# Key-row gathers of a two-layer Perceiver kernel: one transfer per chunk and half, or two of eight heads each

## The reference

```python
x = x + _L0_xattn_ref(_layernorm(x), ctx, mask, ...)   # cross-attention, 4 heads of 64
x = x + _L0_attn_ref(_layernorm(x), ...)               # gated delta net, 12 heads
x = x + _L0_ffn_ref(_layernorm(x), ...)                # 8 experts, top 1
x = x + _L1_xattn_ref(_layernorm(x), ctx, ...)         # cross-attention, 16 heads of 16
x = x + _L1_attn_ref(_layernorm(x), ...)               # linear attention with decay
x = x + _L1_ffn_ref(_layernorm(x), ...)                # 8 experts, top 2
```

## Time and profile before

| | us |
|---|---|
| median of 3 runs | 948.26 (947.57 to 948.73) |
| the profiled execution | 944.76 |
| its span in the profile | 943.0 |
| TensorE matmuls busy | 899.3 (95%) |
| VectorE busy | 704.8 (75%) |
| ScalarE busy | 487.5 (52%) |
| GpSimd busy | 300.1 (32%) |
| HBM read and written | 81.48 and 53.07 MB |

### The profile page before, as it was taken

How to read it: one execution, slowest core, us unless ns; L and a number is a source line. 1 busy time by engine, 2 the same in 40 slices (tenths; PEclk the granted TensorE clock), 3 DMA queues, 4 the chain that set the end, 5 groups by cost and what they waited for, 6 DMA issues and landing times. The chain is left out here.

```text
span 943.0 us, 21457 instructions
## 1 busy us (share of the span) xinstructions
PE 899.3 (95%) x8230; PEld 580.0 (62%) x8230; DVE 704.8 (75%) x1216; ACT 487.5 (52%) x1156; POOL 300.1 (32%) x435
## 2 busy tenths in 40 slices
PE   8999999999999999999999989989999999999987
PEld 5444554455445545567788856666667666776675
DVE  3499888988898889997577448768778788887426
ACT  2543454345434544344583413556667666666742
POOL 5564346434643464445065127201100000000100
PEclk9999999999999999999999979999999999999999
DMA  9467855575356535533300078786666667766000
GB/s 171 171 185 211 250 183 171 143 186 183 104 143 186 180 103 158 132 117 119 134 1 1 1 186 215 203 210 163 163 164 164 163 176 185 177 180 187 5 3 6
DMA packets 103655, 136.33 MB, mean 145 GB/s; under 512 B 64152, under 2 KB 85424, under 8 KB 100880
## 3 DMA queue, kind: packets, MB, share of 16 engines
q1 hardware_dynamic: 99856, 134.22, 52.3%
q10 hardware_dynamic: 3712, 0.92, 0.6%
HBM read 81.48 MB, written 53.07 MB: 143 GB/s over the span
## 5 line engine op out<-in xcount | busy, mean ns | idle before, releaser
L1974 DVE TENSOR_REDUCE mx<-bank 128x1 f32<-128x896 f32 x224 | 232.9, 1086 | 54.6 <-PE bank L1818 53.1
L2035 ACT ACTIVATE p<-bank 128x512 f32<-128x512 f32 x392 | 202.9, 602 | 103.7 <-PE bank L1861 103.4
L704 DVE STREAM_TRANSPOSE ew<-sc 32x896 f32<-32x896 f32 x208 | 229.3, 1102 | 15.3 <-ACT sc L788 7.7
L563 PE MATMUL bank<-Wv,ctxT 128*128 128x512 f32 (+1 forms) x336 | 146.4, 575 | 0.0
L1861 PE MATMUL bank<-home,krows 99*128 99x128 bf16 x1568 | 124.7, 220 | 7.7 <-issue 3.4
L1861 PEld LDWEIGHTS bank<-home,krows 99*128 99x128 bf16 x1568 | 101.3, 98 | 46.4 <-issue 9.9
L1818 PE MATMUL bank<-krows,home 96*128 96x512 bf16 x448 | 123.0, 355 | 1.7 <-DMA krows<-kscr 0.9
L1874 PE MATMUL bank<-p,v 128*32 128x128 f32 x3136 | 108.0, 276 | 3.2 <-issue 3.1
L563 PEld LDWEIGHTS bank<-Wv,ctxT 128*128 128x128 f32 x336 | 63.6, 190 | 71.6 <-issue 64.1
L1874 PEld LDWEIGHTS bank<-p,v 128*32 128x32 f32 x3136 | 80.8, 110 | 31.3 <-ACT p L2035 23.0
L445 POOL CAST kt<-kf 128x512 bf16<-128x512 f32 (+1 forms) x56 | 31.3, 558 | 203.3 <-ACT kf L760 203.3
(11 more groups left out here) (317 smaller groups left out, 1158.1 us busy)
## 6 DMA issues: line engine op xcount, KB each, us to landing
krows<-kscr SPq DMA_DIRECT2D x14, 1536.0 KB, 9.9
krows<-kscr SPq DMA_DIRECT2D x14, 1152.0 KB, 14.7
v<-vscr SPq DMA_DIRECT2D x14, 1004.5 KB, 13.8
vscr<-vpair SPq DMA_DIRECT2D x12, 1004.5 KB, 4.0
kscr<-kt SPq DMA_DIRECT2D x14, 768.0 KB, 3.6
kscr<-kt SPq DMA_DIRECT2D x14, 576.0 KB, 5.1
kscr<-kt SPq DMA_DIRECT2D x14, 512.0 KB, 4.5
ctxB<-ctx SPq DMA_DIRECT2D x56, 112.0 KB, 4.0
```

Of the source, the lines that this page charges most:

```text
L563: ins = pe.matmul(bank[kv_bank(op, s)][:, 0:w * D], turned_context(c)[:, i, k * P:(k + 1) * P], Wv01[:, i, 0:w].rearrange("p w o -> p (w o)"),
L704: dve.transpose(pT0[j * SQ:(j + 1) * SQ, :, :, i * SQ:(i + 1) * SQ].rearrange("m t h q -> m h t q"), rows[:, j]).then_inc(S("turn0"), 1)
L1974: dve.tensor_reduce(mx1[:, c % 2, h:h + 1], psum[:, b:b + 2, :].rearrange("p b n -> p (b n)")[:, 0:CH], AX.X, ALU.max).then_inc(S("smread1 ...
L2035: act.activation(p1[:, g % PR, :], bank[ST1[g % 3]][:], ACT.Exp).then_inc(S("exp1"), 1)
```

## The change

Each gather is issued as two transfers, places 0 to 7 and places 8 to 15 of every row. A partition now gets 8,192 bytes (half 0) or 6,144 bytes (half 1) from each transfer, and the source is read in runs of that length. Both parts raise the same semaphore, so the wait of `score` is for twice the count, and it still waits for all parts of both halves.

```diff
+        GPARTS = 2
+
         def gather(sp, c, half):
 
-            sp.dma_start(krows[half][0:KROWS, c % R1].rearrange("r h m -> r (h m)"),
-                         kscr[half][c].rearrange("j (d h) b m -> (j d) (h b m)", d=D1)
-                         ).then_inc(S(f"krows{half}_{c % R1}"), 16)
+            for part in range(GPARTS):
+                heads = slice(part * H1 // GPARTS, (part + 1) * H1 // GPARTS)
+                sp.dma_start(krows[half][0:KROWS, c % R1, heads].rearrange("r h m -> r (h m)"),
+                             kscr[half][c].rearrange("j (d h) b m -> (j d) (h b) m", d=D1)[:, heads].rearrange("r h m -> r (h m)")
+                             ).then_inc(S(f"krows{half}_{c % R1}"), 16)
...
                 if h == 0:
                     for half in range(2):
-                        pe.wait_ge(S(f"krows{half}_{r}"), 16 * (c // R1 + 1))
+                        pe.wait_ge(S(f"krows{half}_{r}"), 16 * GPARTS * (c // R1 + 1))
```

## The result

Four runs of the changed kernel had a median of 937.22 us (934.23 to 939.84), four of the kernel before beside them 947.91 (947.17 to 948.73): a ratio of 0.9883, with 0.9846 to 0.9919 as its interval of 95%. The prediction had the direction and missed the size: 945.5, range 942.5 to 949.2. The same kernel run again, twelve times beside 25 runs of the kernel before, gave 938.59 (933.94 to 942.8) against 944.43, ratio 0.9936 (0.9913 to 0.9959). The two intervals meet only at their edges, so the median of one batch is not good to its last microsecond here; between 6 and 11 us are gained. Part of the scatter is TensorE's granted clock, which is on record for each run of the second batch: among the 25 runs of the kernel before the time falls by some 0.9 us for each 0.001 that the mean clock is higher, and the changed kernel's twelve got the lower clock (median 0.9895 against 0.991).

A forecast was written before the change was run, and what follows sets the result against it. TensorE work was taken as the chain's largest share by far, with one gather wait and five unnamed stalls to gain from. The first wait (0.9 us) and half the stalls' estimate (1.9) gave 2.8 us less: 945.5 us, range 942.5 to 949.2.

The forecast's parts named there:

- Step 5: TensorE's five unnamed stalls on the chain: shorter traffic and packets save 1.9 us, bounds 0 and 6.2.
- Step 2: Gather packets halved: rate from 15.2 to 25.7 bytes a nanosecond and engine, a pair landing some 4.6 us earlier.
- Step 1: SP's two more issues a pair take 2.1 us, hidden behind its waits: cost 0.
- rival of no change: The split does not speed the packets, slowed by the 96 partitions or the source: 948.3 us; chance 0.14.
- Step 3: TensorE's wait for the first gather pair, before chunk 0's first product, goes: 0.9 us gained, bounds 0 and 1.1.
- Step 4: Other gather and value landings in the chunks come earlier with nobody waiting: gain 0.
- all stalls and the wait: All of TensorE's five stalls and the first wait go, 7.1 us: 941.2 us, left out of the range.
- Only the first wait: Rival: gathers speed up but TensorE's stalls stay or move; 0.9 us gained, 947.4 us; chance 0.26.
- Slower, by the landing: Rival: each extra transfer's own cost makes pairs land 1.9 us later, about 957 us; chance 0.12.
- that page's formula: About 2.0 us fixed per DMA: a 1.5 MB gather 5.6 us, its two halves 7.6 one after the other.

The follow-up runs named there:

- four-part kernel: The changed kernel with each gather in four transfers of four heads, packets of 4,096 and 3,072 bytes: 935.71 us, ratio 0.9893 to the kernel before.
- padded: The kernel before, one transfer per gather, each krows row stored as two groups of eight heads with 8 bytes between: 945.84 us, ratio 0.9996.
- even and odd rows: The kernel before with each gather as two transfers, of its even and its odd rows, packets whole rows: 939.13 us, ratio 0.994.
- six transfers: The kernel before with each gather as six transfers of every sixth row, packets whole rows: 939.12 us, ratio 0.9945.
- the later half: The kernel before with the second gather of each pair held by a later semaphore value, still two transfers a pair: 945.73 us, ratio 1.0003.
- values by columns: The kernel before with the value fetch in two transfers by columns, packets of 4,016 and 4,020 bytes: 945.66 us, ratio 0.9998.
- values from key rows: The kernel before with the value fetch reading from stored key rows 16,384 bytes apart: 944.0 us in a single execution.
- all parts: Four transfers per gather and the value fetch in two by columns, against the kernel before: 935.02 us, ratio 0.9902.
- the worst cut: The kernel before with each gather as two transfers, rows 0 to 47 and rows 48 to 95, packets whole rows: 983.7 us, ratio 1.0386.

## Why the prediction was wrong in size

The step that failed is the fifth, the stalls of TensorE: 1.9 us booked, 6.7 measured. Its reason, shorter packets, failed as well (step 2), and the time that a long stall costs after it has ended, by the clock, was not in the sum at all.

**Step 1, the issues cost nothing: held.** The two more issues made a pair 2.33 us on SP, and SP came to the next issue before its wait was over: it still waited 20.2 us in total for the buffer of the value fetch. The four-part kernel spent 4.70 us a pair and lost nothing either. In front of chunk 0 the fourth part stood in the queue (4.88 us for four) and was in time.

**Step 2, the packets' rate: failed.** 16.7 bytes a nanosecond, not 25.7, and the last landing of the pair came 12.5 us after its issue where it had been 14.7: 2.2 us earlier, not 4.6. The error was one of reading. I laid two lone instruction packets of different queues side by side and took their difference for one of size; and I laid rows on 96 partitions beside rows on 128. The runs held size and partitions apart. Gather packets of 3 to 16 KB whose transfers spanned the 96 partitions all went at 14 to 17 (four parts 15.9, padded 14.2, even and odd rows 17.1, six transfers 14.7); at the same packet size the value rows fell from 26.2 to 13.7 when a transfer wrote 64 contiguous partitions, and the gathers' from 15.2 to 10.0 when it wrote 48 contiguous ones. So the rate goes by the partitions that a transfer spans, and not by the size of its packets in this range. The prediction had named this ("the 96 partitions") under its rival of no change, and gave that 0.14. The Trainium skill, "SBUF — State Buffer", section "Door 1: The DMA port swizzle", says that bandwidth depends on the number of ports that the partitions reach, and that 64 partitions from 0 on reach half of them; the 13.7 against 26.2 agrees. The gathers fit in direction, by the page's mapping: 64 of the 96 rows, and all of rows 0 to 47, lie on one half of the ports.

**Step 3, the first wait: held, in this pair of executions.** 0.88 us gone, the first product right behind the picks. But the wait is not a constant of the old kernel. With the first gathers uncut it was 0.88 us here, 1.7 with the value fetch in partition halves, 1.4 with padded rows, 0.4 with the later half, and absent in four others (no gathers from chunk 3 on, values by columns, values from key rows, no-operations); with even and odd rows 0.3 us were left. On the mean the step is worth less than the 0.9 us booked.

**Step 4, the other landings: held.** Nobody waited for them before or after.

**Step 5, the stalls: the term that was mis-sized, for a reason that fell.** Booked at 1.9 us, it brought 6.7: the long stalls went from 6.19 to 1.39 us, 4.8 less, and 1.7 us more came from the clock, which no longer fell behind the longest stall. The prediction counted what TensorE stands still and nothing for what it then runs at half clock. Across all versions every stretch at the lower level in the chunks began in, or within 2 us of the end of, a stall of 1.55 to 5.47 us: one in the kernel before (and in three of the versions without effect), two with padded rows and with values by columns, three with the value fetch in partition halves, seven with rows 0 to 47 and 48 to 95, and none in the changed kernel's two executions, with four parts, with all parts, with even and odd rows, or without gathers. Not each stall of such length had one: behind the 1.55 us at 740.03 before, the clock stayed full. (Six transfers had one, behind the 2.75 us stall, which is 1.7 of its 285.3 us.) I had set the upper bound at the five long pieces, 6.2, so even the bound was short: without gathers the chunks are 9.0 us shorter. And the halving rested on packet size. One transfer with short packets brought nothing; two or six with long packets brought 6.8 and 5.8 us. By its own steps the forecast could have come to 941.2 (all stalls and the wait), which it put outside its range.

**The sum.** 0.9 + 6.7 = 7.6 us of the 10.5 are the change's; the rest (1.7 ahead of it, 0.15 between the gathers' start and chunk 0, 1.1 behind the chunks) is chance, nearly all of it clock.

**The rivals.** "Only the first wait" leaned on what the Trainium skill ("Runtime: NRT & Kernel Launch", section "Instruction fetch mechanics") says, that the crossing of instruction blocks is mostly hidden. If the stalls are such crossings (argued below), it was not hidden here: 6 us of 291 before, and 31 us in the worst cut. "Slower, by the landing" did not come even with twelve transfers a pair. The Trainium skill's rule to coalesce ("DMA: Bandwidth & Descriptors", section "Rules for kernel authors"), held against the change in the prediction, would have cost 6 to 11 us here. The prediction's test of that page's formula was no test: it laid 5.6 us for one gather beside 11.3 for a pair, and that section of the page is on transfers that GpSimd issues, where these are SP's.

**What is shown and what is open.** Shown: the gathers' price is paid in TensorE's unnamed stalls and in the half clock behind the long ones, 9.0 us in the chunks together. Cutting a gather into more transfers, each of which spans the same partitions from first to last, takes most of it back, whether the packets get shorter or not; cutting by contiguous partitions makes it worse by far. The pace of the pair's issues and a value fetch cut by columns do not matter.

That the stalls are waits for instruction blocks is argued, from single packets of the instruction queue. Of the five stalls before, four end 1.45 to 1.55 us after a 16 KB instruction packet has ended; so do, within 1.4 to 1.8 us, 11 of the 15 in the worst cut and 7 of the 8 with the value fetch in partition halves. The longest stall before, at 617.23, does not fit so well: 0.3 us. And the fetches start later under gather traffic. Measured from the place in TensorE's instruction stream at which the same fetch starts in the kernel without gathers, the 36 fetches are late on the mean by 1.7 to 2.5 us in the versions that gained (2.4 in the changed kernel), by 2.9 to 3.2 in the kernel before and those that gained nothing, and by 3.9 and 4.2 in the two cuts by contiguous partitions.

Not shown is why a block comes sooner when the work ahead of it is cut into more transfers, nor what the longest stall waits for, nor why the partition halves hold blocks up longer; the lower rate of such transfers is the likely part of the last.

## What to carry to other kernels

When an engine's idle time ends in nothing that the profile names and heavy transfers are in flight, try more transfers for the same bytes, cut along the free dimension or by interleaved rows, never by contiguous partitions. Give each stall its own line and its own price before choosing between hidden and not hidden; and leave the traffic out once to learn the ceiling (9.0 us here) before arguing about shares of it. Count with a long stall what the clock takes behind it (1.7 us here after one of 2.36), and look at the granted clock of a stretch before calling a difference in busy time a matter of how it was measured. Two packets that differ in queue, partitions and size are no evidence about size.

## What the runs showed of the hardware that was not expected

- A transfer cut at a contiguous partition boundary is expensive: +39 us for the gathers, +18 us for the value fetch, though bytes and packets stayed. The Trainium skill, "DMA: Bandwidth & Descriptors", section "Rules for kernel authors", says of two transfers to disjoint partition halves not to bother, since they share the same engines; the runs say that they cost.
- A row of a transfer that spans 96 partitions went at 14 to 17 bytes a nanosecond and engine for packets of 3 to 16 KB, one of a transfer to 128 at 26, to 64 contiguous partitions at 13.7, to 48 at 10.0.
- Twenty-four no-operations on SP between two issues did not part them at all.
- Behind long stalls TensorE's granted clock fell, so that they cost more than themselves: it stood at 0.50 from 619.5 to 622.9 us in the kernel before, and in 3.3 us 34 products ran where 61 did at full clock.
- At one place in the program the granted clock differed from execution to execution. Behind the chunks, the kernel before had 0.61 in a stretch where the changed one had full clock, and its 24 products of L2192 (L2196) took 4.57 us in place of 2.94, which is the 1.1 us behind the chunks and more. The windows, before and after:

```profile
912.30:916.70 4.40, 4.39 (x24) 4.40 (x25) 0.69 (x1) 0.09 (x1) 0.00 (x0) 0.61 0.05 5
```

```profile
902.80:906.50 3.70, 3.69 (x33) 3.64 (x33) 0.69 (x1) 0.39 (x2) 0.00 (x0) 1.00 0.07 8
```

  What the engine did just before was nearly the same in both (2.4 us busy, 2 idle, 0.9 busy before the fall). In the second execution of the changed kernel the same place stood at 0.69, so this difference is not the change's.
